# Causal attention on one core: maxima in two pairs of PSUM banks, scores in three single banks, value matmuls in longer groups

## The chip, the cores and the metric

The kernel runs on one core of one Trainium2 chip. The metric is the device time of one execution in microseconds. A core has a matrix engine (TensorE, PE in the profile; its weight loads are PEld), a vector engine (VectorE, DVE), an activation engine (ScalarE, ACT), GpSimd (POOL), and SyncE (SP), which here only starts transfers. The PSUM, into which TensorE writes, has eight banks of 512 float32 columns on 128 partitions.

## The reference

A macaron block on x of shape (1, 4096, 256), all float32:

```
x = x + 0.5 * ffn(layernorm(x))
x = x + attention(layernorm(x))
x = x + 0.5 * ffn(layernorm(x))        # the same weights

ffn(z):       h = z @ W_exp + b_exp             # 256 -> 1024
              h = butterfly(h, up_weights)      # 10 stages of 2x2 mixes
              h = gelu(h + up_bias)             # exact
              h = butterfly(h, down_weights)
              return h @ W_con + b_con + down_bias
attention(z): 16 heads of width 16; scores q.k / 4, causal, softmax, @ v, output projection
```

## The kernel before

The butterflies are folded into two weight matrices at the start. Then come the first feed-forward block with the projections to q, k and v (tiles of 512 tokens), the attention, and the output projection with the second feed-forward block. The change touches the attention alone.

**Softmax in two passes.** The kernel subtracts the true maximum of each row of scores. A first pass computes the scores with queries on partitions and takes their maxima (`maximum`, L1079 on TensorE and L880 on VectorE). A second pass computes the scores again, with keys on partitions (`scores`, L1171); the negated maxima are two extra rows of its operands, so they are subtracted in the matmul. ScalarE takes the exp (`exps`, L672, the instruction of L678) into PB, and `values` (L1189) multiplies by v with a column of ones beside it, which gives the sums. First-pass operands lie on partitions 64 to 111 (NK, NQ), second-pass ones on 0 to 49 (CK, CQ).

**Chunks and slots.** A head has 8 tiles of 512 queries. A chunk is one tile of queries against one tile of 512 keys, and causality leaves 36 chunks (list CH); of each tile the diagonal chunk comes first. TensorE's order is the loop at L1229: slot n handles the scores of chunk n, the values of chunk n-1 and the maxima of chunk n+23 (AHEAD). A chunk has four score matmuls in two halves, four maxima matmuls (M0 to M3 in this text), and two halves of 8 value matmuls; each float32 value matmul is two records, so 16 a half. There are 16 x 36 + 1 = 577 slots, the last with values only. Before, a slot is: M0, two scores, M1, 8 values, M2, two scores, M3, 8 values.

**Banks.** Scores have banks 0 to 3, two to a half. One exp of 1024 columns takes a half, and `scores` waits until the exp of the same half of the chunk before has ended. Maxima go to banks 4, 5 and 7 in turn (MAX_BANKS, `slot_bank`, `slot_free`): a maximum waits for the reduction three places before it. Value sums are in bank 6 (O_BANK), read out by `take_sums` (L683) when a tile of queries ends. PB has two buffers; the exps of a chunk wait for the values of the chunk two before (`pv_done`).

**Row transposes.** Twice a head, `split_step` (L829) makes the maxima of half the head's rows into two parts, and `rows` (L1099) transposes them on TensorE into a bank that takes its own place in the rotation; `take_rows` (L849) copies them out and SyncE moves them into CQ. 31 of these lie in the slots.

**GpSimd** masks the diagonal blocks of the exps (`masks`, L546) and copies v of the next head (`copy_v`, L538). **SyncE** loads the next head's q and k when maxima or scores have passed a chunk (L460 to L487).

Semaphores order the engines, and each engine executes in the order written. The wait of a matmul is on its weight load.

## Time and profile before

| | us |
|---|---|
| median of 3 runs | 2094.49 (2094.09 to 2097.74) |
| the profiled execution, its own time | 2098.32 |
| its span | 2096.6 |
| TensorE busy | 2014.3 |
| VectorE busy | 1665.9 |
| ScalarE busy | 1349.2 |
| GpSimd busy | 257.4 |

The profile gives for each engine the time in which an instruction of it was running. TensorE's matmuls overlap and their ends are modelled, so starts are the surer numbers. PEclk is the granted clock of TensorE as a share of full speed. An "idle before" with a releaser says what ended an engine's idle time; "issue" says that nothing in the profile did.

### The profile page before, as it was taken

To read this page: it belongs to the slowest core of one execution; us is meant where nothing else is said; L and a number is where in the kernel's file an instruction comes from. 1 tells how busy PE (TensorE), PEld (TensorE's weight loads), DVE (VectorE), ACT (ScalarE), POOL (GpSimd) and SP (SyncE) were. 2 spreads that over 40 slices of the span, in tenths; PEclk is the share of its full clock that TensorE was granted. 3 is DMA by queue.
4 is the path that set the end of the run, shared out by engine and by line. 5 is a ranking of instruction groups with operands and counts; after the bars stand their busy time and mean duration, and the time that the engine had idled before them with its cause. 6 is when DMAs were issued, how large, how long until landed. Compare 5 with 4: busy or idle time off the path is not lost.

```text
span 2096.6 us, 58142 instructions
## 1 busy us (share of the span) xinstructions
PE 2014.3 (96%) x23960; PEld 1207.8 (58%) x23960; DVE 1665.9 (79%) x3588; ACT 1349.2 (64%) x1592; POOL 257.4 (12%) x723
## 2 busy tenths in 40 slices
PE   2799999899999999999999999999999999999999
PEld 1667666555555555555555555555555555568887
DVE  7634445379999999999999999999999999636562
ACT  3532222268888888888888888888888888753222
POOL 6400000001111110110111101011111111110000
PEclk9999999999999999999999999999999999999999
DMA  7021111121111111111111111211111111101110
GB/s 203 24 78 66 49 48 48 48 82 42 45 41 44 48 42 46 44 44 44 41 50 46 42 42 40 52 43 44 40 40 51 43 43 32 50 24 61 61 41 21
DMA packets 89977, 104.20 MB, mean 50 GB/s; under 512 B 21264, under 2 KB 52592, under 8 KB 89456
## 3 DMA queue, kind: packets, MB, share of 16 engines
q1 hardware_dynamic: 89008, 100.23, 16.6%
q8 instruction: 190, 3.11, 0.6%
q0 software_dynamic: 704, 0.25, 0.2%
q14 instruction: 75, 0.61, 0.1%
HBM read 70.54 MB, written 29.36 MB: 48 GB/s over the span
## 4 chain that ended last, share of the span: by engine, by line
PE 92%; SPq 2%; DVE 2%; ACT 2%; DMA 1%; issue 1%; ACTq 0%
PE PS L1084 31%; PE PS L1205 31%; PE PS L1061 12%; PE PS L1038 6%; PE PS L1185 6%; PE PS L1136 3%; PE PS L1055 1%; PE PS L1004 1%; SPq L367 1%; DVE MXP L894 1%; DVE OA L782 1%; ACT PG L617 1%; ACT OA L598 0%; SPq L371 0%; ACT L590 0%
## 5 line engine op out<-in xcount | busy, mean ns | idle before, releaser
L678 ACT ACTIVATE PG<-PS 128x1024 f32<-128x1024 f32 (+1 forms) x1152 | 1119.5, 978 | 248.4 <-PE PS L1185 187.1
L894 DVE TENSOR_REDUCE MXP<-PS 128x1 f32<-128x512 f32 x1792 | 1103.9, 685 | 21.6 <-PE PS L1084 20.9
L1084 PE MATMUL PS<-KT,QT 48*128 48x512 f32 (+3 forms) x2304 | 806.3, 431 | 13.7 <-DVE MXP L894 6.4
L1185 PE MATMUL PS<-QT,KT 50*128 50x512 f32 (+1 forms) x2304 | 810.0, 431 | 0.0
L1205 PE MATMUL PS<-PG,VH 128*17 128x128 f32 x16896 | 725.9, 276 | 0.1
L1205 PEld LDWEIGHTS PS<-PG,VH 128*17 128x17 f32 x16896 | 400.1, 96 | 414.4 <-issue 364.0
L1084 PEld LDWEIGHTS PS<-KT,QT 48*128 48x128 f32 x2304 | 340.1, 184 | 267.5 <-issue 139.8
L1185 PEld LDWEIGHTS PS<-QT,KT 50*128 50x128 f32 x2304 | 339.3, 184 | 10.3 <-issue 9.9
L890 DVE CUSTOM_DVE_ANT_0 PS<-PS,MASK 128x128 f32<-128x128 f32 (+3 forms) x512 | 249.2, 505 | 87.8 <-PE PS L1084 81.2
L555 POOL TENSOR_SCALAR_AFFINE_SELECT PG<-PG 128x128 f32<-128x128 f32 x512 | 137.3, 295 | 1005.5 <-ACT PG L678 1005.3
L1061 PE MATMUL PS<-MD,PG 128*128 128x256 f32 x1024 | 234.4, 384 | 1.6 <-ACT PG L617 1.6
L1061 PEld LDWEIGHTS PS<-MD,PG 128*128 128x128 f32 x1024 | 191.7, 191 | 34.5 <-issue 5.9
L617 ACT ACTIVATE PG<-PS,GB 128x512 f32<-128x512 f32 x128 | 86.1, 687 | 189.9 <-PE PS L1038 188.7
L859 DVE TENSOR_TENSOR X<-PS,X 128x256 f32<-128x256 f32 x96 | 40.6, 423 | 176.2 <-PE PS L1061 174.7
L1038 PE MATMUL PS<-XTH,MU 128*128 128x512 f32 x256 | 108.5, 424 | 12.5 <-DVE MUL L826 7.4
L1038 PE MATMUL PS<-XTL,MU 128*128 128x512 f32 x256 | 101.9, 398 | 0.0
L1038 PE MATMUL PS<-XTH,MUL 128*128 128x512 f32 x256 | 101.8, 398 | 0.0
L617 ACT ACT_TABLE_LOAD x17 | 21.8, 1283 | 110.4 <-PE PS L1038 110.3
L528 POOL TENSOR_TENSOR X<-X,OB 128x1024 f32<-128x1024 f32 x16 | 37.7, 2361 | 434.2 <-DVE XN L782 434.1
L890 DVE DVE_READ_ACCUMULATOR2_ANT MXP<- 128x1 f32 x512 | 72.0, 141 | 0.0
L543 POOL COPY VH<-V 128x68 f32<-128x68 f32 x128 | 30.5, 242 | 329.3 <-PE PS L1205 234.2
L1038 PEld LDWEIGHTS PS<-XTH,MU 128*128 128x128 f32 x256 | 49.2, 192 | 35.0 <-issue 12.8
(102 smaller groups left out, 859.5 us busy)
## 6 DMA issues: line engine op xcount, KB each, us to landing
KT<-k_parts SPq DMA_DIRECT2D x256, 64.0 KB
QT<-q_parts SPq DMA_DIRECT2D x256, 64.0 KB
q_parts<-OA SPq DMA_DIRECT2D x16, 512.0 KB, 2.8
k_parts<-OA SPq DMA_DIRECT2D x16, 512.0 KB, 2.7
KT<-k_parts SPq DMA_DIRECT2D x256, 32.0 KB
QT<-q_parts SPq DMA_DIRECT2D x256, 32.0 KB
o_parts<-OS SPq DMA_DIRECT2D x128, 64.0 KB
OA<-o_parts SPq DMA_DIRECT2D x32, 256.0 KB
```

The lines of the kernel that those rows point to most:

```text
L555: nc.gpsimd.affine_select(out=tri, in_=tri, compare_op=ALU.is_ge, fill=0.0, base=0, pattern=[[1, P]], channel_multiplier=-1).then_inc(mask ...
L617: nc.scalar.activation(G[:, b, :], src, ACT.Gelu, bias=GB[:, b:b + 1]).then_inc(gelu_done, 1)
L678: nc.scalar.activation(PB[n % 2][half][:, :, q0:TILE], PS[:, half * 1024:half * 1024 + 1024].rearrange("p (k q) -> p k q", k=2)[:, :, q0:T ...
L859: nc.vector.tensor_tensor(xb, y_bank(b, y), xb, ALU.add).then_inc(y_ev, 1)
L890: nc.vector.tensor_tensor_reduce(out=s, in0=s, in1=MASK[:, 3 * P - qs * P:3 * P - qs * P + w], scale=1.0, scalar=-3e38, op0=ALU.add, op1=A ...
L894: nc.vector.tensor_reduce(dst, bank(b), AX.X, ALU.max).then_inc(mx_red, 1)
L1038: last = mm(dst, w[:, k, b * P:(b + 1) * P].bitcast(f32r), x[:, k, :].bitcast(f32r), start=(k == 0 and x is XTH and w is MU), stop=(k == D ...
L1061: last = mm(y_bank(b, y), lhs[:, k, b * P:(b + 1) * P], rhs[:, k, :], start=(k == 0), stop=(k == nk - 1))
L1084: mm(bank(4 + qs % 2 if b is None else b, w), q[0:SC, (BT * place(j) + qs) * P:(BT * place(j) + qs + 1) * P].bitcast(f32r), k[0:SC, c * TI ...
L1136: last = mm(bank(turn_bank("qk", u)), (WQ if w < 2 else WK)[:, k, (w % 2) * P:(w % 2 + 1) * P], XT2A[:, k, :], start=(k == 0), stop=(k == ...
L1185: last = mm(PS[:, (2 * half + k) * 512 + q0:(2 * half + k + 1) * 512], CK[0:SM, kb * P:(kb + 1) * P].bitcast(f32r), CQ[0:SM, place(j) * TI ...
L1205: last = mm(O_SUM[qs * Q32:qs * Q32 + DV, :], VH[:, c * BT + kb, :], PB[n % 2][half][:, k, qs * P:(qs + 1) * P], start=(j == c and kb == 0 ...
```

## The change

- The scores go to banks 0, 1 and 2 in turn, one at a time (`score_number`). Score g waits for exp g-3. Each score has an exp of its own, of 512 columns (256 in the second half of a diagonal chunk), and counts on one semaphore.
- The value sums move from bank 6 to bank 3.
- The maxima go to the pairs of banks (4, 5) and (6, 7) in turn. M0 of a pair waits for the reduction of the pair two places before. On chunks off the diagonal one reduction of 1024 columns takes a pair (`pair_maximum`); diagonal chunks keep four masked reductions. A row transpose takes the place of a pair.
- The values of a chunk's second half move to the next slot, ahead of the next chunk's first half, except where the chunk is the last of its tile (`ends_tile`). `pv_done` becomes a semaphore for each half.
- Waits: VectorE's clearing of the sums' bank waits for `parts_done` where it waited for the last eviction of v, which TensorE now waits for at its second pair only.

```diff
--- before.py
+++ after.py
@@ -67,8 +67,9 @@
 WO_AT, XT_AT = 18, 28
 O_BUFFERS = 3
 Q32 = 32
-MAX_BANKS = (4, 5, 7)
-O_BANK = 6
+SCORE_BANKS = 3
+PAIR_BANKS = (4, 6)
+O_BANK = 3
 
 
 def w_offset(s):
...
@@ -325,6 +325,10 @@
 
         O_SUM = bank(O_BANK, P)
 
+        def ends_tile(n):
+
+            return CH[n % NCH][1] == 0
+
         def tile_ended(n):
 
             h, n = divmod(n, NCH)
...
@@ -344,16 +348,19 @@
         def slot_items(n):
 
             if n + AHEAD < H * NCH:
-                for qs in range(BT):
-                    yield "max", (n + AHEAD) * BT + qs
+                for half in range(2):
+                    yield "pair", (n + AHEAD) * 2 + half
             for i in rows_in(n):
                 yield "rows", i
 
-        SLOTS = [("rows", 0)] + [i for n in range(SLOT_N) for i in slot_items(n)]
+        SLOTS = [i for n in range(SLOT_N) for i in slot_items(n)]
         SLOT_OF = {item: u for u, item in enumerate(SLOTS)}
 
         def slot_bank(kind, i):
-            return MAX_BANKS[SLOT_OF[kind, i] % 3]
+            return PAIR_BANKS[SLOT_OF[kind, i] % 2] if (kind, i) != ("rows", 0) else PAIR_BANKS[0]
+
+        def score_number(h, n, half, k):
+            return (h * NCH + n) * 4 + 2 * half + k
 
         def inner_weights(eng, src, dst, s, sig):
 
...
@@ -546,10 +553,9 @@
             def masks(h, j):
                 n = CH.index((j, j))
                 for half in range(2):
-                    pool.wait_ge(exp_done[half], h * NCH + n + 2)
-                    pool.sem_inc(passed[0], 1)
                     for k in range(2):
-
+                        pool.wait_ge(exp_done, score_number(h, n, half, k) + 1)
+                        pool.sem_inc(passed[0], 1)
                         kb = 2 * half + k
                         tri = PB[n % 2][half][:, k, kb * P:(kb + 1) * P]
                         nc.gpsimd.affine_select(out=tri, in_=tri, compare_op=ALU.is_ge, fill=0.0, base=0,
...
@@ -666,22 +672,19 @@
                 if t and t != NT - 1:
                     take_v(t - 1)
 
-            act.sem_inc(exp_done[0], 1)
-            act.sem_inc(exp_done[1], 1)
-
             def exps(h, n):
                 j, c = CH[n]
-                act.wait_ge(pv_done, h * NCH + n + 1)
                 for half in range(2):
+                    act.wait_ge(pv_done[half], h * NCH + n + 1)
                     q0 = 2 * P if j == c and half else 0
-                    act.wait_ge(st_ps[half], h * NCH + n + 1)
-                    nc.scalar.activation(
-                        PB[n % 2][half][:, :, q0:TILE],
-                        PS[:, half * 1024:half * 1024 + 1024].rearrange("p (k q) -> p k q", k=2)[:, :, q0:TILE],
-                        ACT.Exp, scale=1.0 / DH ** 0.5).then_inc(exp_done[half], 1)
+                    for k in range(2):
+                        g = score_number(h, n, half, k)
+                        act.wait_ge(st_ps, g + 1)
+                        nc.scalar.activation(PB[n % 2][half][:, k, q0:TILE], bank(g % SCORE_BANKS)[:, q0:TILE],
+                                             ACT.Exp, scale=1.0 / DH ** 0.5).then_inc(exp_done, 1)
 
             def take_sums(h, j):
-                act.wait_ge(pv_done, h * NCH + LAST[j] + 1 + FREE_PB)
+                act.wait_ge(pv_done[1], h * NCH + LAST[j] + 1 + FREE_PB)
                 q = h * NT + RANK[j]
                 if q >= O_BUFFERS:
                     act.wait_ge(os_out[q % O_BUFFERS], 16 * (q // O_BUFFERS))
...
@@ -892,6 +895,20 @@
                                                    accum_out=dst).then_inc(mx_red, 1)
                 else:
                     nc.vector.tensor_reduce(dst, bank(b), AX.X, ALU.max).then_inc(mx_red, 1)
+
+            def pair_maximum(p, n, half):
+
+                j, c = CH[n]
+                b = slot_bank("pair", p)
+                if j == c:
+                    for i in range(2):
+                        maximum(2 * p + i, n, 2 * half + i, b + i)
+                else:
+                    dve.wait_ge(mx_ps, 2 * p + 2)
+                    blk = BT * place(j) + 2 * half
+                    nc.vector.tensor_reduce(MXP[:, blk:blk + 2, c],
+                                            PS[:, b * 512:(b + 2) * 512].rearrange("p (i t) -> p i t", i=2),
+                                            AX.X, ALU.max).then_inc(mx_red, 2)
 
 
             dve.wait_ge(in_bias, 32)
...
@@ -934,17 +951,16 @@
                             dve.wait_ge(at_ps, 2)
                             nc.vector.memset(V[:, :, :, DH:DV], 1.0)
                     residual_stats(t, t)
-            dve.wait_ge(v_ev, NT * BT + FREE_V)
+            dve.wait_ge(parts_done, 4 * NT + FREE_QK)
             nc.vector.memset(O_SUM, 0.0).then_inc(att_init, 1)
 
             for n in range(SLOT_N):
-                for qs in range(BT):
+                for half in range(2):
                     if n + AHEAD < H * NCH:
-                        m = (n + AHEAD) * BT + qs
-                        maximum(m, (n + AHEAD) % NCH, qs, slot_bank("max", m))
+                        pair_maximum((n + AHEAD) * 2 + half, (n + AHEAD) % NCH, half)
                     for i in splits_in(n):
-                        if qs < 3:
-                            split_step(*divmod(i, 2), qs)
+                        for k in range(half, 2 * half + 1):
+                            split_step(*divmod(i, 2), k)
                 for i in rows_in(n):
                     take_rows(i, i % 2)
 
...
@@ -1087,18 +1104,21 @@
             def slot_free(kind, i):
 
                 u = SLOT_OF[kind, i]
-                if u < 2:
-                    pe.wait_ge(mx_red, AHEAD * BT - 1 + u + FREE_MX)
-                elif u > 2:
-                    before, k = SLOTS[u - 3]
-                    if before == "max":
-                        pe.wait_ge(mx_red, k + 1 + FREE_MX)
+                if u == 0:
+                    pe.wait_ge(mt_ev, 1)
+                elif u == 1:
+                    pe.wait_ge(v_ev, NT * BT + FREE_V)
+                else:
+                    before, k = SLOTS[u - 2]
+                    if before == "pair":
+                        pe.wait_ge(mx_red, 2 * k + 2 + FREE_MX)
                     else:
                         pe.wait_ge(mt_ev, k + 1)
 
             def rows(i, grp):
 
-                slot_free("rows", i)
+                if i:
+                    slot_free("rows", i)
                 pe.wait_ge(m_rdy, i + 1)
                 pe.sem_inc(passed[2], 1)
                 nc.tensor.transpose(bank(slot_bank("rows", i), P)[0:PARTS * NB // 2, :],
...
@@ -1164,7 +1184,6 @@
                 if t == NT - 1:
                     v_blocks(t - 1, False)
             pe.wait_ge(parts_done, 4 * NT + FREE_QK)
-            pe.wait_ge(v_ev, NT * BT + FREE_V)
             pe.wait_ge(att_init, 2)
             pe.wait_ge(const_rdy, 2)
 
...
@@ -1179,12 +1198,14 @@
                     if half == 0 and c == j and j == ORDER[g * FIRST_ROWS]:
                         pe.wait_ge(m_ld[g], h * 16 + 16)
                 q0 = 2 * P if j == c and half else 0
-                pe.wait_ge(exp_done[half], h * NCH + n + 1)
                 for k in range(2):
                     kb = c * BT + 2 * half + k
-                    last = mm(PS[:, (2 * half + k) * 512 + q0:(2 * half + k + 1) * 512], CK[0:SM, kb * P:(kb + 1) * P].bitcast(f32r),
-                              CQ[0:SM, place(j) * TILE + q0:(place(j) + 1) * TILE].bitcast(f32r), start=True, stop=True)
-                last.then_inc(st_ps[half], 1)
+                    g = score_number(h, n, half, k)
+                    if g >= SCORE_BANKS:
+                        pe.wait_ge(exp_done, g - SCORE_BANKS + 1)
+                    mm(bank(g % SCORE_BANKS)[:, q0:TILE], CK[0:SM, kb * P:(kb + 1) * P].bitcast(f32r),
+                              CQ[0:SM, place(j) * TILE + q0:(place(j) + 1) * TILE].bitcast(f32r), start=True, stop=True
+                       ).then_inc(st_ps, 1)
 
             def values(h, n, half):
 
...
@@ -1196,7 +1217,7 @@
                         pe.wait_ge(os_ev, q)
                     pe.wait_ge(masked[half], 2 * q + 2)
                 else:
-                    pe.wait_ge(exp_done[half], h * NCH + n + 2)
+                    pe.wait_ge(exp_done, score_number(h, n, half, 1) + 1)
                 if n == K_FIRST[c] and half == 0:
                     pe.wait_ge(vh_rdy[c], h + 1)
                 for k in range(2):
...
@@ -1205,8 +1226,7 @@
                         last = mm(O_SUM[qs * Q32:qs * Q32 + DV, :], VH[:, c * BT + kb, :],
                                   PB[n % 2][half][:, k, qs * P:(qs + 1) * P],
                                   start=(j == c and kb == 0), stop=(c == 0 and kb == (qs if j == c else BT - 1)))
-                if half:
-                    last.then_inc(pv_done, 1)
+                last.then_inc(pv_done[half], 1)
 
             def y_blocks(y, blocks, lhs, rhs, nk):
                 for b in blocks:
...
@@ -1223,21 +1243,24 @@
                     if qs == 0 and k == K_FIRST[c]:
                         pe.wait_ge(ld_nk[c], h * SLICE + SLICE)
                     seq = (n + AHEAD) * BT + qs
-                    slot_free("max", seq)
-                    maximum(seq, k, qs, slot_bank("max", seq))
+                    if qs % 2 == 0:
+                        slot_free("pair", seq // 2)
+                    maximum(seq, k, qs, slot_bank("pair", seq // 2) + qs % 2)
 
             for n in range(SLOT_N):
                 ahead_maximum(n, 0)
                 if n < H * NCH:
                     scores(*divmod(n, NCH), 0)
                 ahead_maximum(n, 1)
+                if n > 1 and not ends_tile(n - 2):
+                    values(*divmod(n - 2, NCH), 1)
                 if n:
                     values(*divmod(n - 1, NCH), 0)
                 ahead_maximum(n, 2)
                 if n < H * NCH:
                     scores(*divmod(n, NCH), 1)
                 ahead_maximum(n, 3)
-                if n:
+                if n and ends_tile(n - 1):
                     values(*divmod(n - 1, NCH), 1)
                 for i in rows_in(n):
                     rows(i, i % 2)
```

TensorE in an ordinary slot before (L1084 maxima, L1185 scores, L1205 values; x7 are the next seven alike):

```order
L1084 MATMUL PS<-KT,QT 128x512 [waits mx_red,ld_nk4]
L1185 MATMUL PS<-QT,KT 128x512 [waits exp_done0]
L1185 MATMUL PS<-QT,KT 128x512
L1084 MATMUL PS<-KT,QT 128x512 [waits mx_red]
L1205 MATMUL PS<-PG,VH 17x128 [waits exp_done0]
L1205 MATMUL PS<-PG,VH 17x128 x7
L1084 MATMUL PS<-KT,QT 128x512 [waits mx_red]
L1185 MATMUL PS<-QT,KT 128x512 [waits exp_done1]
L1185 MATMUL PS<-QT,KT 128x512
L1084 MATMUL PS<-KT,QT 128x512 [waits mx_red]
L1205 MATMUL PS<-PG,VH 17x128 [waits exp_done1]
L1205 MATMUL PS<-PG,VH 17x128 x7
```

And in the changed kernel, where L1101 are maxima, L1206 scores, L1226 values; from the maximum M2 of a slot to the values of the next:

```order
L1101 MATMUL PS<-KT,QT 128x512 [waits mx_red]
L1206 MATMUL PS<-QT,KT 128x512 [waits exp_done] x2
L1101 MATMUL PS<-KT,QT 128x512
L1101 MATMUL PS<-KT,QT 128x512 [waits mx_red]
L1206 MATMUL PS<-QT,KT 128x512 [waits exp_done,ld_ck2]
L1206 MATMUL PS<-QT,KT 128x512 [waits exp_done]
L1101 MATMUL PS<-KT,QT 128x512
L1226 MATMUL PS<-PG,VH 17x128 [waits exp_done]
L1226 MATMUL PS<-PG,VH 17x128 x7
L1226 MATMUL PS<-PG,VH 17x128 [waits vh_rdy3,exp_done]
L1226 MATMUL PS<-PG,VH 17x128 x7
```

There were two groups of 8 values, each behind four matmuls of the other kind; now 16 follow eight such matmuls, and every score has a wait.

TensorE around a row transpose before (L1104), from the values ahead of it:

```order
L1205 MATMUL PS<-PG,VH 17x128 [waits exp_done1]
L1205 MATMUL PS<-PG,VH 17x128 x7
L1104 MATMUL PS<-ident,MP 32x128 [waits mx_red,m_rdy]
L1084 MATMUL PS<-KT,QT 128x512 [waits mx_red,ld_nk3]
L1185 MATMUL PS<-QT,KT 128x512 [waits exp_done0,ld_cq2]
L1185 MATMUL PS<-QT,KT 128x512
L1084 MATMUL PS<-KT,QT 128x512 [waits mx_red]
```

And in the changed kernel (L1124), from the maximum M2 ahead of it:

```order
L1101 MATMUL PS<-KT,QT 128x512 [waits mx_red]
L1206 MATMUL PS<-QT,KT 128x512 [waits exp_done] x2
L1101 MATMUL PS<-KT,QT 128x512
L1124 MATMUL PS<-ident,MP 32x128 [waits mx_red,m_rdy]
L1101 MATMUL PS<-KT,QT 128x512 [waits mx_red,ld_nk3]
L1206 MATMUL PS<-QT,KT 128x512 [waits exp_done,ld_cq2]
L1206 MATMUL PS<-QT,KT 128x512 [waits exp_done]
L1101 MATMUL PS<-KT,QT 128x512
L1226 MATMUL PS<-PG,VH 17x128 [waits exp_done]
```

The transpose lay between values and a maximum; now it lies between two maxima, and the one behind it waits for a reduction as before.

ScalarE across the end of a tile before (L678 exps, L688 the read-out of the sums):

```order
L678 ACTIVATE PG<-PS 128x1024 [waits st_ps1]
L678 ACTIVATE PG<-PS 128x1024 [waits st_ps0,pv_done]
L678 ACTIVATE PG<-PS 128x2x256 [waits st_ps1]
L688 ACTIVATE OS<-PS 128x128 [waits os_out1,pv_done]
L678 ACTIVATE PG<-PS 128x1024 [waits st_ps0,pv_done]
L678 ACTIVATE PG<-PS 128x1024 [waits st_ps1]
L678 ACTIVATE PG<-PS 128x1024 [waits st_ps0,pv_done]
```

And in the changed kernel (L683, L691):

```order
L683 ACTIVATE PG<-PS 128x512 [waits st_ps,pv_done0]
L683 ACTIVATE PG<-PS 128x512 [waits st_ps]
L683 ACTIVATE PG<-PS 128x256 [waits st_ps,pv_done1]
L683 ACTIVATE PG<-PS 128x256 [waits st_ps]
L691 ACTIVATE OS<-PS 128x128 [waits os_out0,pv_done1]
L683 ACTIVATE PG<-PS 128x512 [waits st_ps,pv_done0]
L683 ACTIVATE PG<-PS 128x512 [waits st_ps]
L683 ACTIVATE PG<-PS 128x512 [waits st_ps,pv_done1]
L683 ACTIVATE PG<-PS 128x512 [waits st_ps]
```

Each exp of 1024 columns has become two, which wait one by one.

## Rows read from the trace of the kernel before

**Rows 1.** The page: span, and each engine's busy time, share and instructions.
```profile
span 2096.6 us, 58142 instructions
PE 2014.3 (96%) x23960; PEld 1207.8 (58%) x23960; DVE 1665.9 (79%) x3588; ACT 1349.2 (64%) x1592; POOL 257.4 (12%) x723
```
**Rows 2.** The page: the chain that ended last, by engine and by line.
```profile
PE 92%; SPq 2%; DVE 2%; ACT 2%; DMA 1%; issue 1%; ACTq 0%
PE PS L1084 31%; PE PS L1205 31%; PE PS L1061 12%; PE PS L1038 6%; PE PS L1185 6%; PE PS L1136 3%; PE PS L1055 1%; PE PS L1004 1%; SPq L367 1%; DVE MXP L894 1%; DVE OA L782 1%; ACT PG L617 1%; ACT OA L598 0%; SPq L371 0%; ACT L590 0%
```
**Rows 3.** One line's instructions: ns min/median/max, first and last start in us.
```profile
L1185 PE MATMUL PS<-QT,KT x2304: 274/393/501, 438.2 to 1860.7; 50*128 50x512 f32 x192
...
L1205 PE MATMUL PS<-PG,VH x16896: 272/273/287, 440.9 to 1862.5; 128*17 128x128 f32 x199
```
**Rows 4.** Busy time by stretch: length, us busy of each engine, granted clock.
```profile
core 0: us, PE busy (x) PEld busy (x) DVE busy (x) ACT busy (x) POOL busy (x), PEclk, DMA share, GB/s
...
800.00:1200.00 400.00, 400.00 (x6072) 212.11 (x6061) 383.00 (x826) 325.46 (x362) 47.10 (x180) 1.00 0.17 44
1200.00:1600.00 400.00, 399.99 (x6069) 212.43 (x6069) 381.61 (x834) 325.09 (x359) 47.18 (x181) 1.00 0.17 44
```
**Rows 5.** Timeline of one slot: start and length in us, engine, line.
```profile
1004.54 0.18 PEld L1084 LDWEIGHTS PS<-KT,QT 48*128 48x128 f32 x1 [0.21 <-issue]
1004.54 0.49 PE L1084 MATMUL PS<-KT,QT 48*128 48x512 f32 x1
1004.55 0.49 PE L1185 MATMUL PS<-QT,KT 50*128 50x512 f32 x1
...
1004.88 0.39 PE L1185 MATMUL PS<-QT,KT 50*128 50x512 f32 x1
...
1005.21 0.35 PEld L1205 LDWEIGHTS PS<-PG,VH 128*17 128x17 f32 x16 [0.36 <-issue]
...
1005.37 2.19 ACT L678 ACTIVATE PG<-PS 128x1024 f32<-128x1024 f32 x2 [0.26 <-PE PS L1185]
...
1005.77 0.18 PEld L1084 LDWEIGHTS PS<-KT,QT 48*128 48x128 f32 x1 [0.21 <-issue]
...
1006.99 0.09 PEld L1104 LDWEIGHTS PS<-ident,MP 128*32 128x32 f32 x1 [0.21 <-issue]
```
**Rows 6.** Timeline of the last value matmuls, idle time and releaser in brackets.
```profile
1859.93 2.18 ACT L678 ACTIVATE PG<-PS 128x1024 f32<-128x1024 f32 x2 [0.26 <-PE PS L1185]
...
1860.98 0.79 PEld L1205 LDWEIGHTS PS<-PG,VH 128*17 128x17 f32 x32 [0.36 <-issue]
...
1862.16 0.35 PEld L1205 LDWEIGHTS PS<-PG,VH 128*17 128x17 f32 x16 [0.40 <-ACT PG L678]
```
**Rows 7.** Timeline, VectorE: six reductions back to back.
```profile
1009.18 3.14 DVE L894 TENSOR_REDUCE MXP<-PS 128x1 f32<-128x512 f32 x5 [0.15 <-PE PS L1084]
```
**Rows 8.** Groups by shape: busy us, mean ns of one, idle before.
```profile
L894 DVE TENSOR_REDUCE MXP<-PS 128x1 f32<-128x512 f32 x1792 | 1103.9, 685 | 21.6 <-PE PS L1084 20.9
L678 ACT ACTIVATE PG<-PS 128x1024 f32<-128x1024 f32 x1024 | 1050.0, 1026 | 246.7 <-PE PS L1185 187.1
...
L617 ACT ACTIVATE PG<-PS,GB 128x512 f32<-128x512 f32 x128 | 86.1, 687 | 189.9 <-PE PS L1038 188.7
L678 ACT ACTIVATE PG<-PS 128x512 f32<-128x512 f32 x128 | 76.4, 597 | 1.7
...
L808 DVE CAST XTH<-PS 128x1024 fp32r<-128x1024 f32 x16 | 19.6, 1223 | 21.9 <-PE PS L1004 21.9
```
**Rows 9.** Timeline around a row transpose (L1104), value weights before and after.
```profile
1006.43 0.35 PEld L1205 LDWEIGHTS PS<-PG,VH 128*17 128x17 f32 x16 [0.36 <-issue]
...
1006.99 0.28 PE L1104 MATMUL PS<-ident,MP 128*32 128x128 f32 x1
...
1007.21 0.18 PEld L1084 LDWEIGHTS PS<-KT,QT 48*128 48x128 f32 x1
1007.66 0.18 PEld L1084 LDWEIGHTS PS<-KT,QT 48*128 48x128 f32 x1
...
1008.09 0.35 PEld L1205 LDWEIGHTS PS<-PG,VH 128*17 128x17 f32 x16 [0.25 <-issue]
```

More of the change, by code:

```diff
@@ L988, in _ @@
             pe.sem_inc(y_ps, 1)
-            pe.sem_inc(pv_done, FREE_PB)
+            for half in range(2):
+                pe.sem_inc(pv_done[half], FREE_PB)
             pe.wait_ge(a_up, 1)
```

11 lines of the change are left out of this document (5 added, 6 removed).

## The prediction

> **What bounds the kernel now.** I read the page first. TensorE is busy 96% of the span, VectorE 79%, ScalarE 64% [rows 1], and the chain that ended last is 92% TensorE [rows 2]. The attention runs from the first score at 438.2 us to the last value matmul at 1862.5 us [rows 3]; from 800 to 1600 us TensorE has no idle time at all, at full granted clock, and VectorE is close behind with 383 and 382 of 400 us [rows 4]. So I read the 576 slots of the attention instruction by instruction.
>
> One half of a slot, [rows 5]: a maximum and a score matmul start together at 1004.54, since they lie in different rows of the array. The next two start at 1004.88 (0.34 later: their weights were loaded behind the first two, and one stream is 1004.88 to 1005.10, some 0.22). The value weights load at 1005.21 (0.33 on, of which 0.22 is streaming and 0.11 a pause), and at 1005.77 the next half begins (0.56 for 8 values, pause included). 0.34 + 0.33 + 0.56 = 1.23, and a slot is 1004.54 to 1006.99 = 2.45 us. 576 x 2.45 = 1411, which with the 31 transposes below fills the 1424 us of the stage. Nothing in a slot waits for ScalarE: an exp starts 0.49 after its second score matmul [rows 5] and is needed a whole slot later. What a slot loses is its four switches between the two kinds of matmul, each with a pause of 0.11 and two with a weight load of 0.12 that no stream hides.
>
> **What the change removes.** 28 of the 36 slots of a head put 16 values in a row where there were twice 8 (the 8 others, in which a tile of queries begins, still have a second switch). What 16 in a row cost is seen at the end: the weight loads of 32 records take 0.79 us where 16 take 0.35 [rows 6], so the second 8 cost 0.44 in place of 0.56. And the four matmuls ahead of them now follow others of their kind: 0.22 + 0.22 in place of 0.34 + 0.33. A saving of 0.12 + 0.23 = 0.35 us, a slot of 2.10, and 16 x 28 x 0.35 = 157 us, if nothing waits.
>
> **What it costs.** *VectorE.* Two reductions of 1024 replace four of 512 in an off-diagonal slot. Five back to back take 3.14 with a last one of 0.68 [rows 7], so (3.14 - 0.68) / 4 = 0.61 each, 2.44 a slot. For 1024 the nearest row is a cast of 128x1024 from PSUM, 1223 ns against 685 for 512 [rows 8]: 0.54 more, so 1.15 each, 2.30 a slot. It is hidden if the slot is longer than that.
>
> *ScalarE.* 1024 wide exps of 1.03 us become 512 wide ones. The row for 512 columns (the two-times-256 form of the same line) is 597 ns [rows 8]; four are 2.39 busy, with a little overlap, so also below 2.45. But the **ring** is what counts. Scores now go to three banks in turn, and score g waits for exp g-3. In the new order the four scores between two groups of values come in one burst, two of slot n (call them S2, S3) and two of slot n+1 (S0, S1). S1 takes the bank of S2, which was written only three matmuls earlier. Its weight load waits for that exp, TensorE executes in order, and the maximum and all 16 values behind it wait too. The loop, from one load of S1's weights to the next:
> - load to stream 0.12 (0.34 less a stream of 0.22), stream and pause 0.33 to the value weights, 16 values 0.56 + 0.44: S2's weights load at 1.45;
> - load to stream 0.12, stream start to exp start 0.49 [rows 5]: the exp starts at 2.06;
> - exp 0.60 [rows 8]; end of an activation (1859.93 + 2.18 = 1862.11) to the load that waited for it (1862.16), 0.05 [rows 6]: S1's load at 2.71.
>
> The roundings sum to 0.02 at most and I use 2.70. So an ordinary slot goes from 2.45 to 2.70: 0.35 is saved and 0.60 is waited. ScalarE idles there too; it is latency, not its busy time.
>
> By kind of slot, per head (36 x 2.45 = 88.2 now):
> - 21 ordinary: 21 x 2.70 = 56.7.
> - 7 in which a tile begins behind 16 values: its last 8 values lie between S3 and S0, which hides the exp. From marker to marker 1.45 + 0.34 + 0.33 + 0.56 + 0.34 - 0.12 = 2.90; together 20.3.
> - 7 that follow those, with only 8 values: 0.12 + 0.33 + 0.56, then the loop's 0.12 + 0.49 + 0.60 + 0.05 = 2.27; together 15.9.
> - 1 in which a tile begins behind the tile of a single chunk, with 8 and 8 values: 2.90 - 0.44 = 2.46.
>
> Sum 95.4, +7.2 a head; with the unrounded terms (2.45 is nearer 2.447) +7.0, so +112 us over 16 heads. VectorE's 2.30 is below 2.70 and is hidden at ordinary slots; in the short ones it has two slots of 5.17 for 4.60.
>
> *The row transposes.* 31 times a transpose of the maxima takes a place in the bank rotation. Now it lengthens a half slot from 1.22 to 1.66 (1006.43 to 1008.09) [rows 9], 0.44. With only two pairs in turn, the maxima behind it (ahead of S0) take the bank pair that was filled just before it. Their load waits for that reduction: second matmul of the pair streams at 1.45 + 0.34 = 1.79, reduction starts 0.49 later at 2.28 (0.49 is ScalarE's row, taken for VectorE), takes 1.22 [rows 8], 3.50; +0.05 + 0.34 brings S1's stream to 3.89 where the loop alone gives 2.82. That is 1.07 more, less the 0.44 of now: 0.63 x 31 = +20.
>
> *Small things.* Waits moved from before the first slot to single banks: the exps still come after the same evictions, so nothing. The four output projections and the transposes of the last head lie at slot ends, where S1's wait hides a part: -3. The masks on GpSimd start earlier and have over a slot. SP's queue sees the same loads, released by the same scores.
>
> Sum: +112 + 20 - 3 = +129. The profiled execution took 2098.3 (span 2096.6), the median of the runs is 2094.5; the difference applies to both, 2227 profiled and **2223.5** in the median.
>
> **Rivals.**
> *A, the weight load slips ahead (12%).* If S1's weights are loaded before its wait ends, 0.12 of the loop goes: 28 x 16 x 0.12 = 54, giving 2170. For it: in [rows 5] loads do run ahead of matmuls. Against: in [rows 6] the load itself sits behind the wait and starts 0.05 after ScalarE ends.
> The Trainium skill (TensorE: Matmul & The Clock Gate, section Step-by-step: what each phase is for) says that the queue pulls weight loads ahead of matmuls in flight; by it the time would be this rival's. No row shows it past a wait.
>
> *B, the ring doesn't bind (6%, faster).* Place: S1. If the exp's result came back soon enough, TensorE would run at 2.10 and VectorE's 2.30 would set ordinary slots: 21 x 2.30 + 7 pairs of 4.60 + 2.46 = 83.0 a head, 5.2 less, 83 in all, less the 20 of the transposes: 2031. It decides at the way from S2's load to S1's stream, 0.12 + 0.49 + 0.60 + 0.05 + 0.12 = 1.38: at 0.78 the wait is gone, below 1.13 the change wins. For it: the kernel now shows no wait of a score on an exp. Against: each term has a row, and 0.25 would have to be missing.
> The Trainium skill (TensorEngine Tiling, section Key Properties) says that a change of tiling mode drains the engine. The trace agrees with its pauses of 0.11, and by that page's rule alone, which knows of no ring, the time would be 2094.5 - 157 = 1937.
>
> *C, it does nothing (2%).* The scheduler could give the same order; the listing of the changed order speaks against it, and only gain and wait in balance would leave it at 2094.
>
> Bounds of the unknown sizes: a 512-wide exp could cost like the Gelu of that width, 687 ns [rows 8], +0.09 x 448 = +40, giving 2264; it is nearer to the same line's 597. The reduction could start as much as 0.1 later, +3. Without the wait at the transposes, 20 less.
>
> **Numbers.** 80% for the forecast. The range 2165 to 2250 takes in rival A and most of the longer exp. A measurement of this kernel can tell 0.2%, some 4 us, from no change: slower 0.92, same 0.02, faster 0.06.
>
> **What would show it.** Right: a score's weight load waits for ScalarE about 0.6 us, some 440 times; ordinary slots of 2.70; both TensorE and ScalarE with idle time in each slot; 0.79 for 32 value records; slots of some 3.7 at the transposes; exps of 0.60 and reductions of 1.22; the chain alternating between TensorE and ScalarE. Wrong: slots of 2.58 (A), or VectorE without idle time and slots of 2.30 (B). An exp of 0.6 that starts later than 0.5 after its score would also break the loop's sum.

## The result, and the profile after

| | before | after | ratio |
|---|---|---|---|
| median, us | 2097.74 (5 runs, 2094.09 to 2099.05) | 2262.19 (5 runs, 2260.84 to 2276.97) | 1.0802 (1.0766 to 1.0838) |
| profiled execution, span | 2096.6 | 2275.2 | |

The change makes the kernel 8.0% slower, 164.5 us; the forecast was +129, 6.2%, and its range ended at 2250. The profiled execution is the slowest of the five, 2276.97; the other four lie within 2 us of each other.

The page of the changed kernel, with the lines that answer to [rows 1] and [rows 2], and TensorE's granted clock in forty slices:

```profile
span 2275.2 us, 60124 instructions
...
PE 2078.0 (91%) x23960; PEld 1311.0 (58%) x23960; DVE 1647.9 (72%) x2724; ACT 1382.1 (61%) x2744; POOL 265.5 (12%) x723
...
PEclk8999999899899999999999999999999989999999
...
PE 69%; DVE 14%; ACT 10%; issue 3%; SPq 2%; DMA 1%; ACTq 0%; DVEq 0%
```

TensorE is busy for 91% instead of 96%, and the chain, 92% TensorE before, now passes through VectorE and ScalarE for 14% and 10%. Of TensorE's clock a 9 stands for 90% or more, and two of the four 8s lie in the attention; it was 1.00 from 800 to 1600 us before [rows 4], and the stretches shown with e2 below give it for the attention now.

First and last start of the scores and of the values, answering to [rows 3], and how long the scores' weight loads waited for an exp (us in total, times, longest):

```profile
L1206 PE MATMUL PS<-QT,KT x2304: 275/490/794, 438.2 to 2039.4; 50*128 50x512 f32 x192
...
L1226 PE MATMUL PS<-PG,VH x16896: 272/273/421, 441.1 to 2041.2; 128*17 128x128 f32 x199
...
PEld PS L1206 <- ACT PG L683: 185.2, 396, 0.8
```

The attention runs from 438.2 to 2041.2 us, 179 us longer than before in these two executions. The scores' weight loads waited for an exp 396 times, 0.47 us in the mean. Nothing else of the kernel became longer: the first score starts at 438.2 us as before, and 234 us follow the last values in both.

The groups by shape that the prediction had to take from other rows [rows 8]:

```profile
L683 ACT ACTIVATE PG<-PS 128x512 f32<-128x512 f32 x2048 | 1068.3, 601 | 316.3 <-PE PS L1206 301.5
L909 DVE TENSOR_REDUCE MXP<-PS 128x2 f32<-128x1024 f32 x864 | 1038.1, 1224 | 167.5 <-PE PS L1101 159.5 <-issue 2.9
...
L683 ACT ACTIVATE PG<-PS 128x256 f32<-128x256 f32 x256 | 84.4, 381 | 84.4 <-PE PS L1206 82.3
```

An exp of 512 columns takes 0.60 us and a reduction of 1024 columns 1.22, both as taken. Four reductions behind each other, and an exp with the weight load that waited for it in an ordinary slot (start and length in us):

```profile
1083.29 4.84 DVE L909 TENSOR_REDUCE MXP<-PS 128x2 f32<-128x1024 f32 x4 [0.40 <-PE PS L1101]
...
1088.21 1.08 ACT L683 ACTIVATE PG<-PS 128x512 f32<-128x512 f32 x2 [0.61 <-PE PS L1206]
...
1088.86 0.18 PEld L1206 LDWEIGHTS PS<-QT,KT 50*128 50x128 f32 x1 [0.31 <-ACT PG L683]
```

The reductions are 1.21 apart, (4.84 - 1.22) / 3, where 1.15 was taken. The exp ends at 1088.81, and S1's weights load at 1088.86.

A timeline of one slot, answering to [rows 5], which is also one with a row transpose [rows 9]. Start and length in us, engine and line; L1101 are maxima, L1206 scores, L1226 values, L683 exps, L909 reductions, L1124 the transpose:

```profile
1077.02 0.18 PEld L1206 LDWEIGHTS PS<-QT,KT 50*128 50x128 f32 x1 [0.72 <-ACT PG L683]
...
1077.45 0.79 PEld L1226 LDWEIGHTS PS<-PG,VH 128*17 128x17 f32 x32 [0.24 <-ACT PG L683]
...
1078.45 0.18 PEld L1206 LDWEIGHTS PS<-QT,KT 50*128 50x128 f32 x1
...
1079.08 1.08 ACT L683 ACTIVATE PG<-PS 128x512 f32<-128x512 f32 x2 [0.65 <-PE PS L1206]
1079.16 0.09 PEld L1124 LDWEIGHTS PS<-ident,MP 128*32 128x32 f32 x1 [0.42 <-issue]
...
1079.33 1.23 DVE L909 TENSOR_REDUCE MXP<-PS 128x2 f32<-128x1024 f32 x1 [0.28 <-PE PS L1101]
...
1080.67 0.18 PEld L1101 LDWEIGHTS PS<-KT,QT 48*128 48x128 f32 x1 [1.41 <-issue]
1080.70 0.47 PE L1101 MATMUL PS<-KT,QT 48*128 48x512 f32 x1 [1.24 <-DVE MXP L909]
...
1080.90 0.19 PEld L1206 LDWEIGHTS PS<-QT,KT 50*128 50x128 f32 x1
```

- From S1's weights (1077.02, released by an exp) to the value weights 0.43, 32 value records behind each other 1.00 to S2's weights at 1078.45, 0.63 to its exp at 1079.08: the loop is there with 2.06 for the forecast's 2.06. In ordinary slots S1's weights load 0.05 behind the exp's end, as above, and the slot, from S1's weights to those of the next slot, is 2.69 us in the median.
- The reduction of the pair starts at 1079.33, 2.31 after S1's weights (2.28 forecast). The maximum behind the transpose waits 1.24 us for it, its weights load at 1080.67, and S1's at 1080.90. From S1 to S1 3.88, where 3.77 was forecast; half of the difference is the step from the reduction's end (1080.56) to the weights, 0.11 for 0.05.

The clock was not in the forecast. Stretches of 2.9 to 4.7 us that each hold one slot, S1 to S1, with the granted clock in the third column from the right:

```profile
core 0: us, PE busy (x) PEld busy (x) DVE busy (x) ACT busy (x) POOL busy (x), PEclk, DMA share, GB/s
975.41:979.38 3.97, 2.71 (x41) 1.66 (x43) 3.41 (x8) 2.50 (x5) 0.00 (x0) 1.00 0.22 52
979.38:984.07 4.69, 4.69 (x58) 2.51 (x57) 2.20 (x2) 1.77 (x5) 1.15 (x4) 0.55 0.11 24
984.07:987.62 3.55, 3.55 (x25) 1.66 (x26) 1.70 (x3) 1.99 (x5) 0.00 (x0) 0.50 0.06 18
1077.02:1080.90 3.88, 2.63 (x41) 1.59 (x42) 3.41 (x8) 2.50 (x5) 0.00 (x0) 1.00 0.14 45
1080.90:1083.79 2.89, 2.89 (x58) 1.74 (x59) 1.73 (x2) 1.74 (x4) 0.75 (x3) 1.00 0.14 41
```

At 975.41 and at 1077.02 lies the same slot of two heads, with a transpose, 3.97 and 3.88 us long. Behind the second the clock stays at full and the next slot takes 2.89. Behind the first it falls to half of full speed, the lower of the two levels (1.2 GHz; the mean is 0.55 in the first slot behind it and 0.50 in the second), and the next two slots take 4.69 and 3.55 where 2.88 and 2.39 are usual. TensorE is busy throughout those two slots, so no wait makes them long. In this execution the clock falls behind 13 of the 30 transposes that have such a stall (in the last head nothing waits behind the transpose), and the slots at the lower clock add up to some 42 us more than usual.

### The profile page after: what moved, and what is told of

Read it like the earlier page. It is cut to its first block, busy times and chain, and to the rows that moved or that the text cites. A ratio compares the mean times of both kernels' runs of the same rounds, so it can differ in the third digit from the quotient of the medians.

```text
span 2275.2 us, 60124 instructions
## 1 busy us (share of the span) xinstructions
PE 2078.0 (91%) x23960; PEld 1311.0 (58%) x23960; DVE 1647.9 (72%) x2724; ACT 1382.1 (61%) x2744; POOL 265.5 (12%) x723
## 4 chain that ended last, share of the span: by engine, by line
PE 69%; DVE 14%; ACT 10%; issue 3%; SPq 2%; DMA 1%; ACTq 0%; DVEq 0%
PE PS L1226 22%; PE PS L1101 15%; DVE MXP L909 12%; PE PS L1078 11%; PE PS L1206 10%; ACT PG L683 8%; PE PS L1055 6%; PE PS L1156 3%; PE PS L1072 1%; PE PS L1021 1%; SPq L374 1%; DVE OA L785 0%; ACT PG L623 0%; DVE MXP L897 0%; SPq L393 0%
## 5 line engine op out<-in xcount | busy, mean ns | idle before, releaser
L683 ACT ACTIVATE PG<-PS 128x512 f32<-128x512 f32 (+1 forms) x2304 | 1152.5, 576 | 400.7 <-PE PS L1206 383.8
L909 DVE TENSOR_REDUCE MXP<-PS 128x2 f32<-128x1024 f32 x864 | 1038.1, 1224 | 167.5 <-PE PS L1101 159.5
L1206 PE MATMUL PS<-QT,KT 50*128 50x512 f32 (+1 forms) x2304 | 870.6, 451 | 54.0 <-ACT PG L683 44.1
L1101 PE MATMUL PS<-KT,QT 48*128 48x512 f32 (+3 forms) x2304 | 851.4, 449 | 71.0 <-DVE MXP L909 58.2
L1226 PE MATMUL PS<-PG,VH 128*17 128x128 f32 x16896 | 663.6, 282 | 0.0
L1226 PEld LDWEIGHTS PS<-PG,VH 128*17 128x17 f32 x16896 | 448.6, 99 | 222.4 <-issue 112.4
L1101 PEld LDWEIGHTS PS<-KT,QT 48*128 48x128 f32 x2304 | 375.6, 189 | 343.2 <-issue 245.1
L1206 PEld LDWEIGHTS PS<-QT,KT 50*128 50x128 f32 x2304 | 379.3, 189 | 192.9 <-ACT PG L683 185.2
L893 DVE CUSTOM_DVE_ANT_0 PS<-PS,MASK 128x128 f32<-128x128 f32 (+3 forms) x512 | 242.8, 513 | 116.6 <-PE PS L1101 114.4
L561 POOL TENSOR_SCALAR_AFFINE_SELECT PG<-PG 128x128 f32<-128x128 f32 x512 | 146.8, 292 | 1107.7 <-ACT PG L683 1105.1
L1055 PEld LDWEIGHTS PS<-XTH,MU 128*128 128x128 f32 x256 | 49.1, 192 | 35.4 <-issue 13.7
```

The source lines that it names most:

```text
L561: nc.gpsimd.affine_select(out=tri, in_=tri, compare_op=ALU.is_ge, fill=0.0, base=0, pattern=[[1, P]], channel_multiplier=-1).then_inc(mask ...
L683: nc.scalar.activation(PB[n % 2][half][:, k, q0:TILE], bank(g % SCORE_BANKS)[:, q0:TILE], ACT.Exp, scale=1.0 / DH ** 0.5).then_inc(exp_don ...
L893: nc.vector.tensor_tensor_reduce(out=s, in0=s, in1=MASK[:, 3 * P - qs * P:3 * P - qs * P + w], scale=1.0, scalar=-3e38, op0=ALU.add, op1=A ...
L909: nc.vector.tensor_reduce(MXP[:, blk:blk + 2, c], PS[:, b * 512:(b + 2) * 512].rearrange("p (i t) -> p i t", i=2), AX.X, ALU.max).then_inc ...
L1055: last = mm(dst, w[:, k, b * P:(b + 1) * P].bitcast(f32r), x[:, k, :].bitcast(f32r), start=(k == 0 and x is XTH and w is MU), stop=(k == D ...
L1101: mm(bank(4 + qs % 2 if b is None else b, w), q[0:SC, (BT * place(j) + qs) * P:(BT * place(j) + qs + 1) * P].bitcast(f32r), k[0:SC, c * TI ...
```

## The experiments

All medians are against the kernel before on the same chip, 2097.46 to 2099.07 us.

**e1: the old order of the values.**

```diff
                 ahead_maximum(n, 1)
-                if n > 1 and not ends_tile(n - 2):
-                    values(*divmod(n - 2, NCH), 1)
                 if n:
                     values(*divmod(n - 1, NCH), 0)
...
-                if n and ends_tile(n - 1):
+                if n:
                     values(*divmod(n - 1, NCH), 1)
```

> The changed kernel with the order of the values as it was (8 values behind each four matmuls), so the new banks and single exps alone. Theory (the wait of score g on exp g-3 costs time only where four scores come in one burst): between two scores of a burst of two and the next two there are 8 values, so no score waits; only the row transposes stay longer, +0.4 us x 31 = +12, about 2108 us, granted clock near 1.00, slots of 2.45 us. Rival (the ring of three banks, the single exps or the paired reductions cost time wherever they are): well above 2150 us.

Measured 2122.00, ratio 1.0124 (1.0109 to 1.0139), granted clock 0.99. Ordinary slots are 2.45 us. So the three score banks, the single exps and the paired reductions cost nothing in an ordinary slot, and 140 of the 164.5 us need the moved values. The rest is at the transposes, and it is twice what was expected: their slots take 3.5 to 3.6 us where 2.45 + 0.44 + 0.4 = 3.3 was. The stall that lengthens them, in a slot with a transpose:

```profile
1015.37 0.47 PE L1101 MATMUL PS<-KT,QT 48*128 48x512 f32 x1 [0.74 <-DVE MXP L909]
```

TensorE's matmuls stand idle for 0.74 us at each of 30 transposes, where they stand for 1.24 in the changed kernel, and the clock falls behind none of them.

**e2: no row transposes in the slots.** Their places in the rotation, TensorE's `rows` and VectorE's copies go; a count stands in for the copy, and the buffer that it would have filled is cleared once. The negated maxima of later heads stay at old values.

```diff
-            for i in rows_in(n):
-                yield "rows", i
...
+            nc.vector.memset(MROW[1][:, :], 0.0)
...
                 for i in rows_in(n):
-                    take_rows(i, i % 2)
+                    dve.sem_inc(mt_ev, 1)
...
-                for i in rows_in(n):
-                    rows(i, i % 2)
```

> The changed kernel without the 31 row transposes in the slots, their copies and their places in the rotation of the bank pairs. This leaves the negated maxima of later heads at old values. Theory (what the forecast missed is TensorE's clock, which falls to half behind the long stalls at the transposes): granted clock back at 0.99 as before the change, attention 2.70 us per ordinary slot and none above 2.9, about 2095 + 97 = 2192 us. Rival (the clock falls because TensorE waits 0.6 us in every slot): granted clock stays near 0.97, about 2192 + 35 = 2227 us.

Measured 2195.10, ratio 1.0471 (1.0454 to 1.0489). The stretches from 500 to 1800 us of the changed kernel, and of this one, with the columns as above:

```profile
500.00:1000.00 500.00, 464.33 (x6688) 268.14 (x6682) 413.62 (x637) 367.15 (x752) 53.88 (x196) 0.96 0.16 39
1000.00:1500.00 500.00, 463.57 (x6774) 268.66 (x6766) 421.77 (x644) 373.74 (x767) 56.15 (x204) 0.98 0.15 40
1500.00:1800.00 300.00, 278.93 (x4010) 161.15 (x4008) 248.79 (x383) 220.67 (x453) 31.86 (x116) 0.95 0.16 39
```

```profile
500.00:1000.00 500.00, 474.42 (x7090) 276.37 (x7094) 436.95 (x672) 390.22 (x801) 56.61 (x206) 1.00 0.16 41
1000.00:1500.00 500.00, 474.37 (x7088) 276.25 (x7078) 436.48 (x667) 389.46 (x800) 57.47 (x210) 1.00 0.16 41
1500.00:1800.00 300.00, 284.46 (x4258) 165.72 (x4258) 262.54 (x393) 233.95 (x481) 34.77 (x126) 1.00 0.17 42
```

The clock is back at 1.00, and the rival is out: the loop's 0.6 us in every ordinary slot does not lower it. In these stretches no idle time between matmuls is longer than 0.38 us. The time is 3 us above the 2192 expected. The waits of this kernel (us in total, times, longest; L1205 are its scores) show the loop:

```profile
PEld PS L1205 <- ACT PG L681: 191.8, 425, 0.7
```

425 weight loads, with 28 x 16 = 448 foreseen; the idle time of 0.45 and the load of 0.12 that no stream covers are the 0.60 of the prediction, nearly.

**e5: work while TensorE waits.** Three matmuls of 256 columns behind each transpose; the wait for the reduction stays.

```diff
+FILL = 3
...
                 for i in rows_in(n):
                     rows(i, i % 2)
+                    g = 4 * (n + 1)
+                    pe.wait_ge(exp_done, g - SCORE_BANKS + 1)
+                    for _ in range(FILL):
+                        mm(bank(g % SCORE_BANKS)[:, 0:2 * P], ident[:, :], WO[:, 0, :], start=True, stop=True)
```

> The changed kernel with three extra matmuls of 256 columns (1.3 us together) behind each row transpose, written to the score bank that is overwritten next, so that TensorE streams while it would stand waiting for the reduction. They remove no wait. Theory (clock falls behind the stall): the granted clock rises from 0.97 towards 0.99, the slots of 3.8 at the transposes stay, the slots of 3.5 to 4.7 behind them go, about 2228 us, 35 us less than the changed kernel although work is added. Rival (the long slots behind the transposes are waits for data of their own): 2262 us or more.

Measured 2236.87, ratio 1.0670 (1.0648 to 1.0692): 25 us less than the changed kernel, by added work. The same stretches, and then a slot with a transpose and the next:

```profile
500.00:1000.00 500.00, 474.44 (x6964) 278.65 (x6962) 428.79 (x657) 381.26 (x780) 54.99 (x200) 1.00 0.16 40
1000.00:1500.00 500.00, 475.15 (x6978) 279.42 (x6978) 429.04 (x660) 380.83 (x780) 56.66 (x206) 1.00 0.16 40
1500.00:1800.00 300.00, 284.96 (x4171) 167.38 (x4171) 257.20 (x400) 228.18 (x467) 33.47 (x122) 1.00 0.16 41
```

```profile
1257.01:1260.89 3.88, 3.87 (x47) 2.57 (x48) 3.40 (x8) 2.50 (x5) 0.00 (x0) 1.00 0.18 45
1260.89:1263.77 2.88, 2.88 (x58) 1.74 (x58) 1.72 (x2) 1.74 (x4) 0.74 (x3) 1.00 0.20 44
```

The transpose's slot is still 3.88, as in the changed kernel, and the one behind it 2.88. Only TensorE's idle time is gone (3.87 of 3.88 busy), and the granted clock is 1.00. So the long slots behind a transpose were clock, and the clock's price is 2262.19 - 2236.87 = 25 us in the median, some 5 us either way by e5's interval alone. In the changed kernel's profiled execution it was more: its mean granted clock is 0.967 where the other four have 0.974 to 0.976, it took 15 us above the median, and 42 us fall to the slots at the lower clock.

**e4 and e7: the loop's exp made shorter**, in the changed kernel and in e2.

```diff
-                        nc.scalar.activation(PB[n % 2][half][:, k, q0:TILE], bank(g % SCORE_BANKS)[:, q0:TILE],
+                        nc.scalar.activation(PB[n % 2][half][:, k, q0:q0 + 2 * P], bank(g % SCORE_BANKS)[:, q0:q0 + 2 * P],
```

> The changed kernel with every exp of 512 columns cut to its first 256 (the other half of the probabilities is left out). Only the latency of the exp changes. Theory (the loop score, exp, fourth score sets the ordinary slot): exp 0.38 in place of 0.60, ordinary slots 2.48 in place of 2.70, 28 x 16 x 0.21 = 94 us less than the changed kernel at the least, about 2165 us, less where the clock recovers too. Rival (the slot is set by VectorE's two reductions of 1024 or by TensorE itself): within 15 us of the changed kernel's 2262.

> The changed kernel without the row transposes in the slots and with every exp cut to 256 columns (old negated maxima, half of the probabilities left out). Theory (the loop through the exp alone sets the ordinary slot): 2195 - 448 x 0.21 = 2101 us. Rival (with the exp 0.21 us shorter VectorE's two reductions, 2.30 us a slot in bursts, are the next bound already): ordinary slots of 2.5 to 2.6 us and 2110 to 2125 us.

e4 measured 2204.38, ratio 1.0511 (1.0495 to 1.0527), 58 less than the changed kernel, granted clock 0.965. e7 measured 2122.93, ratio 1.0124 (1.0108 to 1.0141), 72 less than e2. The exp of e4, by shape:

```profile
L683 ACT ACTIVATE PG<-PS 128x256 f32<-128x256 f32 x2304 | 763.2, 382 | 721.3 <-PE PS L1206 704.9
```

The exp became 0.22 shorter and ordinary slots 2.52 us at full clock, in the median, in place of 2.70. Shortening the exp shortens the slot, so it is in the loop; but the full 94 us did not come in either. In e7, where the clock plays no part, VectorE (third pair of figures) is busy 91%:

```profile
1000.00:1500.00 500.00, 483.51 (x7420) 284.56 (x7416) 455.71 (x690) 274.85 (x841) 60.26 (x220) 1.00 0.16 43
1500.00:1800.00 300.00, 289.69 (x4456) 170.88 (x4452) 272.49 (x428) 164.16 (x502) 36.83 (x136) 1.00 0.16 42
```

e7 came out inside its rival's range, 2110 to 2125, and its ordinary slots are 2.51 us, 0.09 above VectorE's two reductions of 1.21. That fits the rival, by which the reductions come next: from e2 to e7 the scores' weight loads wait less for exps (191.8 us, then 72.7) and those of the maxima more for reductions (73.2, then 92.1). No run takes this part alone. e4's smaller gain fits its clock, 0.965 to 0.969 in its four executions against 0.974 to 0.976 in the changed kernel: it falls behind 16 of 30 stalls of 0.95 to 1.04 us.

**e3 and e8: the transposes' price elsewhere**, the edit of e2 made in the kernel before and in e1.

> The kernel before the change without its 31 row transposes in the slots (the negated maxima of later heads stay at old values). It gives the price that the transposes had before. Theory: 0.44 us each, 14 us less than before, about 2083 us. Rival (they were hidden): no change.

> The changed kernel with the old order of the values and without the row transposes in the slots (old negated maxima). Theory (of the new banks and single exps only the transposes cost anything): 2097.5 - 14 = 2083 us, the same as the kernel before without them. Rival (the single exps or three banks cost by themselves): 2095 us or more.

e3 measured 2086.60, ratio 0.9946 (0.9932 to 0.9960); e8 2086.50, ratio 0.9946 (0.9933 to 0.9959). Both are some 3.5 us above the 2083 expected, as a transpose cost 0.35 us before and not 0.44, and both are the same: without transposes the new banks and the single exps are worth nothing either way. The 31 transposes cost 2097.5 - 2086.6 = 11 us before the change, 2122.0 - 2086.5 = 35.5 with the pairs in the old order (1.15 each), and 2236.9 - 2195.1 = 42 with the pairs and the moved values, the clock left out.

**e6: the values' move alone**, on the kernel before.

```diff
                 ahead_maximum(n, 1)
+                if n > 1 and not ends_tile(n - 2):
+                    values(*divmod(n - 2, NCH), 1)
                 if n:
                     values(*divmod(n - 1, NCH), 0)
...
-                if n:
+                if n and ends_tile(n - 1):
                     values(*divmod(n - 1, NCH), 1)
```

with `pv_done` a semaphore for each half, as in the change.

> The kernel before the change with the move of the values alone: 16 values in a row, but scores in four banks with exps of 1024 columns and maxima in three single banks. Theory (a burst of eight matmuls holds four maxima, and with three single banks and 0.61 us a reduction the fourth waits for the first one's reduction; the values' move needs more maxima banks): ordinary slots about 2.75, some 2215 us. Rival (with no ring of three scores the saving of 0.35 us a slot comes through): below 2060 us.

Measured 2201.02, ratio 1.0493 (1.0477 to 1.0508), against 2215 expected. The weight loads of maxima waited for reductions (L1088 are its maxima; us in total, times, longest):

```profile
PEld PS L1088 <- DVE MXP L897: 225.1, 685, 2.3
```

Its scores hardly wait for an exp, 15 times and 4.5 us in all. So the move needs banks on both sides. With four score banks the maxima stall it, with four maxima banks the scores do, and eight banks are all there are.

**e9, e10 and e11: the transposes out of the rotation.** The transpose writes the score bank that comes next, and its copy goes ahead of VectorE's next reduction. The core of e9, on e1:

```diff
-            return [i for i in range(1, 2 * H) if split_slot(i) + 1 == n]
+            return [i for i in range(1, 2 * H) if split_slot(i) + 2 == n]
...
+        def rows_score(i):
+            return (split_slot(i) + 2) * 4 + 2
...
-                    slot_free("rows", i)
+                    pe.wait_ge(exp_done, rows_score(i) - SCORE_BANKS + 1)
...
+                        if g == rows_score(i):
+                            pe.wait_ge(mt_ev, i + 1)
...
                 ahead_maximum(n, 1)
+                for i in rows_in(n):
+                    rows(i, i % 2)
```

> The changed kernel with the old order of the values, and the row transposes complete but in another place: one slot later, behind M1, into the score bank that is written next, their copy ahead of VectorE's next reduction, and out of the rotation of the bank pairs. Theory (the transposes cost by their place in the rotation, where the next maximum waits for a reduction of 1024 columns): only one more switch on TensorE is left, 0.2 us x 31 = 6, about 2093 us, less than before. Rival (they cost the same wherever they lie): about 2097 us or more.

> The changed kernel, values in its own order, with the row transposes complete and placed as in e9. Theory: the stall behind them goes and with it the fall of the clock, so 2195 + 7 = 2202 us at a granted clock of 0.99. Rival (the presence of a transpose, not the stall, lets the clock fall): granted clock 0.97 and 2225 us or more.

e9 measured 2142.49, ratio 1.0203 (1.0175 to 1.0231); e10 2234.19, ratio 1.0651 (1.0630 to 1.0671). The theory missed both, and in e9 the rival, the same cost wherever they lie, is no explanation either. In e9 the transpose itself (L1126) does what was meant, 0.21 us between values and what was ahead, and its copy (L859) comes at once:

```profile
1065.14 0.09 PEld L1126 LDWEIGHTS PS<-ident,MP 128*32 128x32 f32 x1 [0.37 <-issue]
...
1065.35 0.35 PEld L1231 LDWEIGHTS PS<-PG,VH 128*17 128x17 f32 x16
...
1065.46 0.28 DVE L859 COPY MROW<-PS 32x128 f32<-32x128 f32 x1
```

What was lost begins with a later wait, at the first slot of the next head. The transpose had been moved a slot later, its rows go through a DMA into the queries' tile, and the head's first score now waits for it:

```profile
1073.86 0.18 PEld L1211 LDWEIGHTS PS<-QT,KT 50*128 50x128 f32 x1 [1.65 <-issue]
1073.89 0.47 PE L1211 MATMUL PS<-QT,KT 50*128 50x512 f32 x1 [1.37 <-DMA QT<-MROW]
```

TensorE idles 1.37 us there. Fourteen heads start late in this way, by 0.7 to 1.9 us, 20 us in all. Behind three of them, not the one shown, the clock fell, and those slots cost some 26 us more (0.977 over the span); the transposes themselves cost 7. e10 has the same waits, 12 us of them, and three falls of the clock worth 12 us. All three come behind a head's late start (1.37, 1.58 and 1.70 us of idle) and none behind a transpose, so its rival is out too, although its 2225 us or more came true. e11 moves the transposes back, to behind M3 of the old slot:

```diff
-            return [i for i in range(1, 2 * H) if split_slot(i) + 2 == n]
+            return [i for i in range(1, 2 * H) if split_slot(i) + 1 == n]
...
-            return (split_slot(i) + 2) * 4 + 2
+            return (split_slot(i) + 2) * 4
...
                 ahead_maximum(n, 3)
+                for i in rows_in(n):
+                    rows(i, i % 2)
```

> As e9, but each transpose one and a half slots earlier: behind M3 of the slot where it was, ahead of the values, into the score bank that the next slot's S0 takes; the copy lies between VectorE's two reductions of that slot. Complete computation. Theory (in e9 each transpose cost only 0.21 us, and the rest was the wait of a head's first score for the row transfer, made late): no slot above 2.7, granted clock 0.99, 2086.5 + 31 x 0.21 = 2093 us, 4 less than before the change. Rival (the long slot at a head's start is caused by something else than the transfer's lateness): above 2120 us again.

Measured 2095.38 in 12 runs against 2098.91 in 17, ratio 0.9987 (0.9977 to 0.9997), with a complete computation; 2093 was expected, and a slot with a transpose takes 2.66. It is faster than both kernels; than the one before by 0.13% only, with an interval that just clears 1. From 500 to 1800 us:

```profile
500.00:1000.00 500.00, 499.90 (x7611) 263.57 (x7607) 477.15 (x721) 434.63 (x859) 61.89 (x224) 1.00 0.18 45
1000.00:1500.00 500.00, 499.74 (x7593) 263.67 (x7592) 476.05 (x737) 433.81 (x857) 62.95 (x227) 1.00 0.19 44
1500.00:1800.00 300.00, 299.85 (x4557) 158.22 (x4556) 285.24 (x420) 260.63 (x515) 36.86 (x133) 1.00 0.17 43
```

TensorE has no idle time to speak of, as before the change, and VectorE is at 95%. e10's changed order would need the same repair; it was not tried.

## Why the prediction was wrong, point by point

The direction, the main mechanism and its size were right, and the range was missed by 12 us. The term that failed is TensorE's clock, which the forecast put at nothing; the transposes were mis-sized beside it. The runs split the 164.5 us:

| term | forecast | measured | from |
|---|---|---|---|
| loop through S1's bank, slots of 2.70 | +112, and -3 | +108.5 | e2 less e3 |
| row transposes, above their price before | +20 | +31 | (e5 less e2) less (before less e3) |
| TensorE's clock | 0 | +25 | changed kernel less e5 |

The result is 39 us above the forecast of 2223.5: 25 of clock, 11 of transposes, and 3 because the forecast started from a median of 2094.5, where five runs of the kernel before have 2097.74.

- *What bounds the kernel*: right. Ordinary slots of 2.45 were TensorE's alone.
- *The saving of 0.35 a slot*: of it 0.12 stands in the rows after (1.00 for 16 values in place of 1.12). The other 0.23, of the eight matmuls in a row, lies under the longer wait. It rests on a stream of 0.22, for which the prediction had no row; the shortest time from one score to the next is 0.23 in e2. The shortest ordinary slots of e6, where scores hardly wait, are 2.13 for the forecast's 2.10.
- *The ring*: right in place, mechanism and size, 2.69 to 2.70 measured for 2.70. The other kinds of slots came to 2.76, 2.39 and 2.43 for 2.90, 2.27 and 2.46 (the first two follow each other, 5.15 for 5.17, so their errors cancel). The sum of the kinds is 7.15 a head or +114, and an old slot of 2.447 makes it larger; the prediction's step down to +112 is not founded.
- *Durations of unseen shapes*: 0.60 and 1.22, as taken. The reductions' distance was 1.21 and not 1.15, so that VectorE's two take 2.42 a slot and not 2.30; below 2.70 this cost nothing.
- *The row transposes*: mechanism right, mis-sized. The price in the changed kernel was put at 0.44 + 0.63 = 1.07 each and is 42 / 31 = 1.35; that of before was put at 0.44 and was 0.35. The slot itself was 3.88 for 3.77, and the slot behind it is 0.12 longer as well, which the sum left out.
- *"At full granted clock"*: this is the step that failed. The prediction read the clock of the kernel before and carried it over. It foresaw idle time of over 1 us at the transposes on top of 0.6 in each slot, and counted only the wait. Behind some of these stalls (13 of 30 in the profiled execution) TensorE ran slots at half clock: 25 us in the median. With such a term in it the forecast would have been 2249, 14 us below the result.
- *The bound of 2264*: it lies next to the result by chance. It was the price of an exp of 0.69 us, and the exp took 0.60.
- *Rival A*: out, the weight load starts 0.05 behind the exp. The Trainium skill (TensorE: Matmul & The Clock Gate, section Step-by-step: what each phase is for) says that weight loads are pulled ahead of matmuls in flight; here the load of 1088.86 was not pulled ahead of its own wait.
- *Rival B*: out here, and too cheap at 2.30 a slot; e7 suggests that with a shorter exp VectorE's reductions take over part of the slot.

## What to carry to other kernels

When work is merged into longer groups to save switches, count what each group must hold in buffers on both sides of it: here a ring of three served bursts of two without a wait and stalled bursts of four by 0.6 us, since the round trip to the consumer came into the slot. Follow each wait to the instruction that frees the buffer and add up the loop; the longest loop is the new period whatever any engine's busy share says. And where a forecast puts idle time on TensorE, ask of the clock behind it too, with a term of its own in the range.
